# Two routed feed-forward layers: token rows gathered tile by tile through an inverted slot table, instead of scattered into slots and gathered back

## What is computed

```python
def _L0_ffn_ref(hidden_states, Wr, W1, b1, W2, b2):      # 8 experts, inner width 1024
    router_probs = jax.nn.softmax(x @ Wr, axis=-1)
    expert_idx = jnp.argmax(router_probs, axis=-1)        # one expert for each token
    ...
    outs = gelu(x @ w1 + bb1) @ w2 + bb2                  # of every expert
    return max(router_probs) * outs[of expert_idx]

def _L1_ffn_ref(X, W1, b1, W3, b3, W2, b2, Wg, bg, Wf, bf):   # 8 experts, inner width 512
    gating = jax.nn.softmax(X @ Wg + bg, axis=-1)
    top_k_indices = jnp.argsort(gating, axis=-1)[..., -2:]    # two experts for each token
    h = jax.nn.silu((X @ W1 + b1) * (X @ W3 + b3))
    mixed = sum of gating[k] * (h @ W2 + b2)[k] over the two
    return mixed @ Wf + bf
```

## Time and profile before

| | |
|---|---|
| median of 3 runs | 3436.51 us (3435.71 to 3441.28) |
| profiled execution, first to last instruction (span) | 3429.7 us |
| median less span | 6.8 us |
| busy in the span: PE, DVE, ACT, POOL | 85%, 55%, 41%, 18% |

### The profile page before, as it was taken

One profiled execution on the slowest core, in us unless ns is written; L12 is line 12 of the kernel. 1 busy time (PEld: TensorE's weight loads), 2 busy tenths in 40 slices (PEclk: granted clock), 3 DMA queues, 4 the chain that ended last, 5 costly groups with the idle time before them and its releaser, 6 DMA issues. The chain is left out here.

```text
span 3429.7 us, 46832 instructions
## 1 busy us (share of the span) xinstructions
PE 2900.1 (85%) x13932; PEld 2111.7 (62%) x13933; DVE 1886.9 (55%) x3558; ACT 1407.8 (41%) x2923; POOL 608.0 (18%) x571
## 2 busy tenths in 40 slices
PE   6495879972898798999789999999999998355997
PEld 5495545532786487999556666666666665233664
DVE  4312555403454336444478888888888886352332
ACT  1141544420221114444447777776777776100110
POOL 0202111113102120000201111111111111144554
PEclk7698889985998598999889999999999999577998
DMA  1443010005222101000010001000011000425775
GB/s 37 168 144 96 1 27 14 14 1 217 84 99 77 35 1 50 25 24 0 10 28 21 22 14 35 14 21 20 15 25 24 22 14 2 168 81 152 173 172 134
DMA packets 158692, 195.46 MB, mean 57 GB/s; under 512 B 39057, under 2 KB 129320, under 8 KB 154952
## 3 DMA queue, kind: packets, MB, share of 16 engines
q1 hardware_dynamic: 122072, 131.88, 12.8%
q0 software_dynamic: 22192, 40.13, 4.9%
q10 hardware_dynamic: 14304, 22.02, 1.9%
HBM read 105.38 MB, written 67.80 MB: 50 GB/s over the span
## 5 line engine op out<-in xcount | busy, mean ns | idle before, releaser
L1849 ACT ACTIVATE l3a_pt_hi<-l3a_banks 128x512 fp32r<-128x512 f32 (+2 forms) x640 | 382.0, 597 | 316.7 <-PE l3a_banks L1795 253.8
L1956 DVE TENSOR_TENSOR l3a_pt_lo<-l3a_pt,l3a_pt_hi 128x512 fp32r<-128x512 f32 (+2 forms) x640 | 460.3, 724 | 90.5 <-ACT l3a_pt L1850 85.9
L1850 ACT ACTIVATE l3a_pt<-l3a_banks 128x512 f32<-128x512 f32 (+2 forms) x640 | 378.0, 591 | 0.0
L1930 DVE TENSOR_REDUCE l3a_maxima<-l3a_banks 128x1 f32<-128x1178 f32 x256 | 351.4, 1376 | 2.4 <-PE l3a_banks L1746 1.1
L1795 PE MATMUL l3a_banks<-l3a_pt_hi,l3a_v 128*65 128x512 f32 (+2 forms) x640 | 286.3, 447 | 7.7 <-ACT l3a_out L1864 7.7
L1805 PE MATMUL l3a_banks<-l3a_q,l3a_k 128*128 128x512 f32 (+2 forms) x640 | 256.8, 401 | 7.2 <-ACT l3a_pt L1850 3.3
L1806 PE MATMUL l3a_banks<-l3a_q,l3a_k 72*128 72x512 f32 (+5 forms) x640 | 253.6, 396 | 0.0
L1795 PE MATMUL l3a_banks<-l3a_pt_hi,l3a_v_lo 128*65 128x512 f32 (+2 forms) x640 | 252.6, 395 | 0.0
L1795 PE MATMUL l3a_banks<-l3a_pt_lo,l3a_v 128*65 128x512 f32 (+2 forms) x640 | 252.4, 394 | 0.0
L1746 PE MATMUL l3a_banks<-l3a_k,l3a_q 128*128 128x512 f32 (+1 forms) x768 | 216.2, 392 | 15.4 <-DVE l3a_maxima L1930 14.3
L1746 PEld LDWEIGHTS l3a_banks<-l3a_k,l3a_q 128*128 128x128 f32 x768 | 141.8, 195 | 61.6 <-DVE l3a_maxima L1930 39.3
(11 more groups left out here) (524 smaller groups left out, 6053.1 us busy)
## 6 DMA issues: line engine op xcount, KB each, us to landing
l3f_w<-in_L_ffn_w SPq DMA_DIRECT2D x96, 256.0 KB, 3.2
l0f_w<-in_L_ffn_W ACTq DMA_DIRECT2D x12, 1024.0 KB, 6.6
l3f_slots_x<-l3f_empty SPq DMA_DIRECT2D x10, 1168.0 KB, 14.3
l3f_x_rows<-l3f_slots_x SPq DMA_DIRECT2D x32, 292.0 KB, 3.9
l1f_w<-in_L_ffn_W ACTq DMA_DIRECT2D x18, 512.0 KB, 4.6
l2f_w<-in_L_ffn_w SPq DMA_DIRECT2D x16, 512.0 KB, 4.7
l3a_q<-l3a_q SPq DMA_DIRECT2D x64, 128.0 KB, 2.3
l3a_k<-l3a_k SPq DMA_DIRECT2D x64, 128.0 KB, 2.3
```

Of the source, the lines that this page charges most:

```text
L1849: act.activation(a.pt_hi[0:rows, n % a.pt_slots, :], a.st_bank[0:rows, n % 2, :], ACT.Exp, bias=bias, scale=scale)
L1850: act.activation(a.pt[0:rows, n % 4, :], a.st_bank[0:rows, n % 2, :], ACT.Exp, bias=bias, scale=scale).then_inc(a.exped, 1)
L1930: dve.tensor_reduce(a.maxima[:, n:n + 1], banks.rearrange("p a b -> p (a b)")[:, 0:KEYS], AX.X, ALU.max).then_inc(a.maxed, 1)
L1956: dve.tensor_tensor(a.pt_lo[0:rows, slot, :], a.pt[0:rows, n % 4, :], a.pt_hi[0:rows, slot, :].bitcast(F32), ALU.subtract).then_inc(a.lo_m ...
```

## The change

The rows of `chip.xn` go to a plain copy `rows` in DRAM, in token order, by four transfers of SP during the routing, with one tile of zero rows behind them. `show_slots`, `invert_slots` and `token_table` make the inverse of `place`: a table that tells for each slot of each tile which token row sits there (an empty slot gets a zero row). VectorE builds one-hot matrices, TensorE multiplies them, and in L1 a second such product (`weights_inverted`) gives the weight of each slot.

In the loop SP does nothing any more. POOL fetches the next x tile by an indirect transfer whose indices are a column of the table (`in_index`), and writes `y_tile` to token rows of `sums` by an indirect transfer with another column (`out_index`): a plain write in L0, where each token has one slot, and a read-add-write (`compute_op=ALU.add`) in L1, where it has two. In L1 VectorE weights y ahead of that (`y_sum`, then `y_tile`). Behind the loop SP reads `sums` back by four plain transfers. In L1 the mixing on VectorE and the bias matmul of ones are gone: x gets the bias (`gbf`) ahead of the loop, and TensorE turns one tile ahead (`turn_mixed`).

The routing steps are reordered a little, so that the weights are worked out while TensorE counts ranks. The diff, cut to its core (L0 first, L1 where it differs):

```diff
+def show_slots(dve, step, sem, place, slot, lane, column, lanes, columns, ids, at_column, of_token, at_lane):
+    entries, width = place.shape[1], columns.shape[1]
+    step(dve.tensor_copy(slot, place))
+    step(dve.tensor_scalar(lane, slot, P - 1, None, ALU.bitwise_and))
+    step(dve.tensor_scalar(column, slot, 7, None, ALU.logical_shift_right))
+    step(dve.tensor_tensor(at_column, spread(column, width), columns.unsqueeze(1).to_broadcast([P, entries, width]), ALU.is_equal))
+    step(dve.tensor_tensor(of_token, at_column, spread(ids, width), ALU.mult))
+    for n in range(0, entries, TABLE_CHUNK):
+        dve.tensor_tensor(at_lane[:, n:n + TABLE_CHUNK, :], spread(lane[:, n:n + TABLE_CHUNK], P),
+                          lanes.unsqueeze(1).to_broadcast([P, TABLE_CHUNK, P]), ALU.is_equal).then_inc(sem, 1)
+def invert_slots(pe, out, at_lane, values, ready=None):
...
+        ins = pe.matmul(out, at_lane[:, n, :], values[:, n, :], start=n == 0, stop=n == entries - 1)
 def l0_ffn(nc, chip, I):
...
-            for slots in (slots_x, slots_y):
...
+            sp.dma_start(rows[TOKENS:TOKENS + P, :], zeros[:]).then_inc(rows_kept, 16)
+            load_expert(sp, 0, 0)
+            for q in range(4):
+                sp.wait_ge(turn.staged, 4 * (q + 1))
+                sp.dma_start(rows[4 * q * P:4 * (q + 1) * P, :].rearrange("(t p) d -> p t d", p=P), chip.xn[:, 4 * q:4 * (q + 1), :]
+                             ).then_inc(rows_kept, 16)
...
-                    sp.wait_ge(x_turned, at)
-                    sp.dma_start(x_tile[:], slots_x[bass.ds(at * P, P), :]).then_inc(x_loaded, 16)
+            sp.wait_ge(all_stored, 1)
+            for q in range(4):
+                sp.dma_start(fetched[:, 4 * q:4 * (q + 1), :], sums[4 * q * P:4 * (q + 1) * P, :].rearrange("(t p) d -> p t d", p=P)
+                             ).then_inc(fetched_part[q], 16)
...
-            for t in range(TILES):
-                pool.indirect_dma_start(slots_x, bass.IndirectOffsetOnAxis(index[:, t:t + 1], 0), chip.xn[:, t, :], None
-                                        ).then_inc(scattered, 16)
+            pool.indirect_dma_start(x_tile[:], None, rows, bass.IndirectOffsetOnAxis(table[:, 0:1], 0)).then_inc(x_loaded, 16)
             g = one_register(pool, "l0f_pool_g")
             with pool.Fori(0, E) as e:
                 with tiles_of_expert(pool, tile_counts, e, g, MAX_TILES) as at:
+                    pool.wait_ge(indexed, at)
+                    pool.sem_inc(taken, 1)
+                    pool.indirect_dma_start(x_tile[:], None, rows, bass.IndirectOffsetOnAxis(in_index[:], 0)).then_inc(x_loaded, 16)
                     pool.wait_ge(y_kept, at + 1)
-                    pool.dma_start(slots_y[bass.ds(at * P - P, P), :], y_tile[:]).then_inc(y_stored, 16)
+                    pool.sem_inc(taken, 1)
+                    pool.indirect_dma_start(sums, bass.IndirectOffsetOnAxis(out_index[:], 0), y_tile[:], None).then_inc(y_stored, 16)
                     pool.wait_ge(y_stored, at * 16)
                     pool.sem_inc(y_free, 1)
...
 def l1_ffn(nc, chip, I):
...
+                    pool.wait_ge(y_kept, at)
+                    pool.sem_inc(taken, 1)
+                    pool.indirect_dma_start(sums, bass.IndirectOffsetOnAxis(out_index[:], 0), y_tile[:], None,
+                                            compute_op=ALU.add).then_inc(summed, 16)
+                    pool.wait_ge(summed, at * 16)
...
+            for t in range(0, TILES, 4):
+                dve.tensor_tensor(chip.x[:, t:t + 4, :], chip.x[:, t:t + 4, :], gbf[:].unsqueeze(1).to_broadcast([P, 4, D]), ALU.add
+                                  ).then_inc(biased, 1)
...
+                    dve.tensor_tensor(y_sum[:], p_y[:, 0:D], tile_of(b2, e), ALU.add).then_inc(y_summed, 1)
+                    dve.wait_ge(y_summed, at + 1)
                     dve.wait_ge(y_free, at)
-                    dve.tensor_tensor(y_tile[:], p_y[:, 0:D], tile_of(b2, e), ALU.add).then_inc(y_kept, 1)
+                    dve.tensor_copy(out_index[:], column(table, at - 1))
+                    dve.tensor_scalar(y_tile[:], y_sum[:], column(weight_table, at - 1), None, ALU.mult).then_inc(y_kept, 1)
```

More of the change, by code:

```diff
@@ L500, in one_register, with table_constants, token_table @@
     return g
+TABLE_CHUNK = 8
+def table_constants(pool, sem, lanes, columns, ids):
+    iota = dict(allow_small_or_imprecise_dtypes=True)
+    pool.iota(lanes, [[1, P]], base=0, channel_multiplier=0).then_inc(sem, 1)
+    pool.iota(columns, [[1, columns.shape[1]]], base=0, channel_multiplier=0).then_inc(sem, 1)
+    pool.iota(ids, [[0, ids.shape[1] // TILES], [P, TILES]], base=-TOKENS, channel_multiplier=1, **iota).then_inc(sem, 1)
+def show_slots(dve, step, sem, place, slot, lane, column, lanes, columns, ids, at_column, of_token, at_lane):
[9 more added lines that the diff above has]
+def invert_slots(pe, out, at_lane, values, ready=None):
+    entries = at_lane.shape[1]
+    for n in range(entries):
+        if ready is not None and n % TABLE_CHUNK == 0:
+            pe.wait_ge(ready, n // TABLE_CHUNK + 1)
+        ins = pe.matmul(out, at_lane[:, n, :], values[:, n, :], start=n == 0, stop=n == entries - 1)
+    return ins
+def token_table(dve, step, sums, own, spare, table):
+    step(dve.scalar_tensor_tensor(spare, sums, 0.0, own.to_broadcast([P, sums.shape[1]]), ALU.is_equal, ALU.mult))
+    step(dve.scalar_tensor_tensor(table, sums, float(TOKENS), spare, ALU.add, ALU.add))
 def l0_ffn(nc, chip, I):
@@ L620, in _ @@
             turn_rows(16)
+            pe.wait_ge(placed, 1)
             g = one_register(pe, "l0f_pe_g")
@@ L681, in _ @@
             dve.wait_ge(exped, 1)
+            dve.wait_ge(constants, 7)
+            choose(dve, step, exps[:], chosen[:], order[:], place[:], best[:], 0)
+            dve.sem_inc(chose, 1)
             step(dve.tensor_reduce(weight[:], exps[:], AX.X, ALU.add))
@@ L692, in _ @@
             expert_bases(dve, step, chip.ones, rank[:], upto[:], compare[:], thresholds[:], tiles[:], ends[:], tile_counts[:])
-            slots_dve(dve, step, rank[:], chosen[:], product[:], place[:], index[:])
+            step(dve.tensor_tensor(product[:], chosen[:], rank[:].rearrange("p e t -> p t e"), ALU.mult))
+            step(dve.tensor_reduce(place[:], product[:], AX.X, ALU.add))
+            show_slots(dve, step, lanes_shown, place[:], slot[:], lane[:], column_of[:], lanes[:], columns[:], ids[:], at_column[:], of_token[:], at_lane[:])
+            dve.wait_ge(inverted, 1)
+            token_table(dve, step, p_route[:, 384:384 + SLOT_TILES], own[:], spare[:], table[:])
+            dve.sem_inc(tabled, 1)
             dve.sem_inc(placed, 1)
@@ L700, in keep_turned @@
                 dve.tensor_copy(xt_tile[:], p_xt[:, 0:D]).then_inc(x_kept, 1)
+                dve.tensor_copy(in_index[:], column(table, turnings)).then_inc(indexed, 1)
             keep_turned(1)
@@ L731, in l1_ffn @@
         b13_rows, b13 = sb("b13_rows", [2 * E * FC, P]), sb("b13", [P, 2 * E * FC])
[L732 to L735, removed]
+        b2, bg, gbf = sb("b2", [P, E, D]), sb("bg", [P, E]), sb("gbf", [P, D])
+        zeros = sb("zeros", [P, 4, D])
@@ L759, in l1_ffn @@
         w_loaded = [sem("w_loaded0"), sem("w_loaded1")]
-        gathered = [sem(f"gathered{q}") for q in range(TILES // 2)]
+        indexed, taken = sem("indexed"), sem("taken")
+        mixed_part = [sem(f"mixed{q}") for q in range(4)]
         block = stack.enter_context(nc.Block())
[L762 to L767, removed]
@@ L793, in _ @@
-            g = one_register(sp, "l1f_sp_g")
-            with sp.Fori(0, E) as e:
-                with tiles_of_expert(sp, tile_counts, e, g, MAX_TILES) as at:
-                    sp.wait_ge(x_turned, at)
-                    sp.dma_start(x_tile[:], slots_x[bass.ds(at * P, P), :]).then_inc(x_loaded, 16)
+            sp.dma_start(rows[TOKENS:TOKENS + P, :], zeros[:, 0, :]).then_inc(rows_kept, 16)
+            load_expert(sp, 0, 0)
+            for q in range(4):
+                sp.wait_ge(turn.staged, 4 * (q + 1))
+                sp.dma_start(rows[4 * q * P:4 * (q + 1) * P, :].rearrange("(t p) d -> p t d", p=P), chip.xn[:, 4 * q:4 * (q + 1), :]
+                             ).then_inc(rows_kept, 16)
@@ new lines, in _ @@
+            load_expert(sp, 1, 1)
+            for q in range(4):
+                sp.dma_start(sums[4 * q * P:4 * (q + 1) * P, :].rearrange("(t p) d -> p t d", p=P), zeros[:]).then_inc(based, 16)
+            sp.dma_start(sums[TOKENS:TOKENS + P, :], zeros[:, 0, :]).then_inc(based, 16)
+            sp.wait_ge(all_summed, 1)
+            for q in range(4):
+                sp.dma_start(mixed[:, 4 * q:4 * (q + 1), :], sums[4 * q * P:4 * (q + 1) * P, :].rearrange("(t p) d -> p t d", p=P)
+                             ).then_inc(mixed_part[q], 16)
```

229 lines of the change are left out of this document (120 added, 109 removed).

## The result

The changed kernel takes 3785.86 us (median of 4 runs, 3779.45 to 3796.72) where the kernel before took 3438.9: a ratio of 1.1015, 95% interval 1.0995 to 1.1035, 347 us more by the medians. The profiled execution took 3785.48 us, its span is 3783.8, so 354.1 more than the span before. So of the 6.8 us between span and median before, some 5 are not start and end of an execution: the execution that was profiled there was that much shorter than the median run.

What follows compares the result with a forecast made beforehand. TensorE bounds the loops before; afterwards a wait cycle through POOL's fetches and y landings does. Loops add 122 (L0) and 288 (L1), gains take 99: +311 on span 3429.7, with 6.8 around it 3748 us, range 3610 to 3820.

Steps and rivals of the forecast that it cites:

- The gains: Ahead of and behind both loops: 15.7 and 10.7 us less in L0, 28 and 44.5 in L1, together 99.
- The end of L1: Behind L1's loop: 36.7 us instead of 81.2, 44.5 less, with the clock rising after two tiles.
- The ring: Both loops: next x fetch waits for previous y landing; rounds 11.3 us against 7.32 (L0), 11.4 against 5.84 (L1).
- so I take half the rounds: L0's loop: clock falls in half the rounds at 2.6 us a fall, so 12.6 us a round on average.
- the second rival: L0's loop: clock falls in every round, 13.9 us each; in all +336, 3773 us; chance 0.23.
- Weights and changes of expert: Both loops: six weight loads add 18 us in L0, 12 in L1; seven expert changes add 4 in each.
- the first: Both loops: clock stays at the upper level through the gaps, rounds 11.3 and 11.4 us; 3652 us; chance 0.27.
- The faster one: Both loops: the x fetch stays hidden, only gains and some 10 us of longer y steps count; 3348 us; chance 0.03.

Runs made afterwards that it cites:

- E3: Changed kernel with x fetched one tile further ahead and SyncE waiting for the y landings, both layers: 3334.86 us, ratio to before 0.9691.
- E1: Changed kernel with POOL's fetch of x one tile further ahead in both layers: 3387.45 us, ratio to before 0.9853.
- E2: Changed kernel with SyncE instead of POOL waiting for the y landing and freeing the y tile, fetch left in place: 3572.76 us.
- E6: Changed kernel with L1's y rows written plainly, the add taken out (leaves out the sum over a token's two experts): 3741.89 us.
- E5: Changed kernel with unread extra matmuls ahead of the wait for x, 8 in L0 and 12 in L1: 3719.47 us.
- E7: Changed kernel with both loops keeping the first two experts' weights, the other six not loaded: 3728.46 us.
- E4: Changed kernel with unread extra matmuls ahead of the wait for x, 14 in L0 and 20 in L1: 3796.11 us.

## Why the prediction was right, and where its sizes were off

**The gains** came in sum as worked out: 103.6 us by the first, third, fourth and sixth row of the table, against 99; E3's stretches give 101.7. The parts did not. The end of L1 gave 5.7 more than I took: its tiles came 1.08 us apart at the upper clock, not 1.4. Against `place` the first turns came 13.1 and 25.5 us earlier, where the prediction names some 16 and 31. In L1 its sum had 4.8 (3.0 + 1.8) for inverting the weights; TensorE took 7.2 for that alone, at a granted clock of 0.50. That L1's row still came to 27.8 is luck in part: the stretch ahead of `place` was 3.7 shorter than before (I had taken 1.9), and it varies between 485.9 and 492.3 in the nine profiles.

**The ring** is there, link by link. L0: VectorE 0.42, start 0.82 (I took 0.6), landing 2.4, restart 1.17 (1.0), gather 2.82 (2.7), turn to addition with the index copy 5.87: 13.50. L1: VectorE 0.35 and 0.68, start 0.82, landing 3.7, restart 1.19, gather 2.76, TensorE 4.24: 13.74. E1, E2 and E3 show that it is the order and not the transfers: each edit that took links out of the ring took their time out of the round. E6 shows the landing in it.

**The step that failed in L0** is "so I take half the rounds". Every round pays. In one-us stretches of the plain L0 round above (columns as before), the clock is up through the gap, falls 0.25 us after TensorE starts to turn the x tile (172.41), and is up again shortly after 176:

```profile
170.00:171.00 1.00, 0.00 (x0) 0.00 (x0) 0.00 (x0) 0.00 (x0) 0.56 (x1) 1.00 0.00 0
...
172.00:173.00 1.00, 0.59 (x3) 0.59 (x4) 0.06 (x1) 0.00 (x0) 0.00 (x0) 0.83 0.00 0
173.00:174.00 1.00, 1.00 (x4) 0.73 (x4) 0.43 (x2) 0.00 (x0) 0.00 (x0) 0.50 0.00 0
...
176.00:177.00 1.00, 1.00 (x6) 0.82 (x6) 0.00 (x0) 0.00 (x0) 0.00 (x0) 0.96 0.00 0
```

That is the mechanism of the second rival (the prediction calls it the third in one place), and its 3773 lies nearer to 3786 than the forecast's 3748. A fall costs 1.7 there and not the 2.6 I priced: the clock was low for 3.4 us, not 5.1. The Trainium skill, TensorE: Matmul & The Clock Gate, section HAM oscillation — how this bites in real kernels, describes such a loop: the clock is reduced in the wait for a transfer and the next burst starts at the lower level, each time. The trace agrees for L1, where TensorE starts to turn at 0.50 in all 36 rounds, and for twelve rounds of L0; in the other seven of L0 the clock is still up then and falls 0.1 to 0.9 us later. At the upper clock the ring is 11.8 and 11.95 (E5), 0.5 longer than my 11.3 and 11.4. So a plain round is mostly 13.46 instead of 12.6 in L0 and 13.75 instead of 13.4 in L1: 16 and 13 of the 38 us by which the forecast of 3748 was short.

**Weights and changes of expert in L0** were mis-sized: 22.6 and some 11.5 (267.3 less 19 x 13.46) instead of 18 and 4, 12 us more. Of the 11.5, some 8 are POOL's restart at the seven changes of expert, 1.1 each and 1.4 at the first where I took 0.6, and the rest is the clock, down for longer in some rounds; the forecast's term had no such part. In L1 the two together came to 16, as taken. The gains gave some 5 back.

**The rivals.** The clock held in no round of either loop, so the first (3652) is out, and E5 prices what it would have given back. The faster one (3348) needed the fetch to be issued ahead of the previous landing; E3 does that, and gives 3335.

**The remainder** of 5.8 us lies behind L1's last row, in stages that no edit touches: 2262.4 before, 2268.2 now. In the nine profiles that stretch takes 2261.0 to 2274.8, so it is no more than their spread.

## What to carry to other kernels

Fusing a gather and a scatter into a loop moves waits onto one in-order queue: write down, for the loop's queue, which issue stands behind which wait, and add up the ring before counting what the fusion saves. Here the same transfers took 3786 us in all behind a landing, and 3335 with the fetch one tile ahead and the landing awaited on an idle engine. A gap in TensorE's work is to be priced twice, as the gap and as the slower matmuls behind it, here 1.7 to 1.8 us a round.

## What the runs showed of the hardware that was not expected

- In the changed kernel the six y writes of L0 issued just behind 2 MB of weight loads landed 6.0 to 6.5 us after their start, the others in 2.4; without the loads (E7) all took 2.4. In E1 such a landing and the restart behind it left POOL idle for 7.84 us.
- The clock can fall after the work has come back: in the L0 round shown it read 1.00 through a gap of 4.35 us and 0.50 from 173. In E2, L0 rounds with and without a fall stand side by side (11.2 and 9.5).
- An indirect gather issued 1.29 us behind an indirect write of POOL landed in 2.8 us, as long as one alone takes (E2, plain rounds of L0); with weight loads beside them it took 5.6 to 5.9.
- A float32 product of 128x128 and 128x256 takes two rows of 0.22 us on TensorE, 0.45 in all (E4: 28 rows, 6.21).
